# An adaLN layer (linear attention, then an int8-style FFN) on eight cores: row round trips moved to GpSimd's queue, staged weight pieces consumed in another order, FFN scales turned by TensorE

## The reference

```python
mod = (silu(c) @ wmod).reshape(8, 6, 1, 1024)
sa, ca, ga, sb, cb, gb = mod[:, 0], ..., mod[:, 5]
ga = (2 * (ga >= 0) - 1) * max(|ga|, 0.25)          # gb likewise
h = layernorm(x) * (1 + ca) + sa
q = relu(h Wq^T) / 8 ; k = relu(h Wk^T) / 8 ; v = h Wv^T ; u = silu(h Wu^T)   # 16 heads of 64
o = srms_norm(q @ (k^T v)) * u                      # k^T v summed over all 2048 tokens
x = x + ga * (o Wo^T)
h = layernorm(x) * (1 + cb) + sb
# per-token int8 quantization of h, per-row int8 quantization of the FFN weight, integer matmul
x = x + gb * ((h_q Wf_q^T) * h_scale * w_scale + bias)
```

## Time and profile before

| what | value |
|---|---|
| median of 3 runs | 490.98 us (487.46, 490.98, 512.98) |
| the profiled execution, its own time | 486.76 us |
| its span, slowest core (5) | 484.3 us |
| spans of the 8 cores | 467.4 to 484.3 us |
| PE busy | 397.9 us (82%) |
| DVE busy | 279.1 us (58%) |
| ACT busy | 231.4 us (48%) |
| POOL busy | 80.8 us (17%) |
| HBM read, written | 70.36 MB, 24.67 MB |

### The profile page before, as it was taken

How to read it: one execution, slowest core, us unless ns; L and a number is a source line. 1 busy time by engine, 2 the same in 40 slices (tenths; PEclk the granted TensorE clock), 3 DMA queues, 4 the chain that set the end, 5 groups by cost and what they waited for, 6 DMA issues and landing times.

```text
span 484.3 us, 6412 instructions; the slowest of 8 cores (467.4 to 484.3 us)
## 1 busy us (share of the span) xinstructions
PE 397.9 (82%) x2052; PEld 185.2 (38%) x2052; DVE 279.1 (58%) x492; ACT 231.4 (48%) x327; POOL 80.8 (17%) x136
## 2 busy tenths in 40 slices
PE   3234499999999982878978199989999989998994
PEld 0121244455454440324433044434344434444441
DVE  3565751647206656478557256556476645765885
ACT  4342153764662310776486253374844467643431
POOL 3222310515000000000022002121122122022321
PEclk9985789999999995989999789998999999999999
DMA  7999899593996999979999605634526554265787
GB/s 224 272 279 278 212 203 294 220 292 127 231 244 203 320 301 271 204 213 387 355 110 125 162 0 88 131 67 108 87 65 122 120 88 104 72 130 89 92 140 158
DMA packets 21185, 87.03 MB, mean 180 GB/s; under 512 B 4257, under 2 KB 4257, under 8 KB 16290
## 3 DMA queue, kind: packets, MB, share of 16 engines
q1 hardware_dynamic: 13666, 58.33, 39.5%
q0 software_dynamic: 7488, 28.31, 34.4%
HBM read 70.36 MB, written 24.67 MB: 196 GB/s over the span
## 4 chain that ended last, share of the span: by engine, by line
PE 38%; DMA 30%; DVE 11%; ACT 9%; issue 8%; SPq 2%; POOL 1%; DVEq 0%; ACTq 0%; POOLq 0%
PE pb L360 33%; DMA rows<-ws_c 7%; DMA wa<-wmod_a 7%; DMA stage<-wmod_b 5%; DMA row_g<-rows 5%; DMA xr<-x_tm 4%; DVE stage L427 3%; SPq L46 2%; ACT rn L677 2%; ACT osq L667 2%; PE pb L386 2%; PE pb L675 1%; ACT xq L777 1%; DVE wm_c L485 1%; DMA silr<-rows 1%
## 5 line engine op out<-in xcount | busy, mean ns | idle before, releaser
L360 PE MATMUL pb<-wo_s,u_s 128*128 128x512 bf16 x256 | 62.5, 398 | 1.4 <-DVE u_s L657 1.4
L360 PE MATMUL pb<-fq,xqT 128*128 128x512 bf16 x256 | 60.1, 379 | 2.6 <-ACT xqT L789 2.3
L360 PE MATMUL pb<-h,wq_s 128*128 128x512 bf16 x256 | 61.6, 385 | 0.0
L360 PE MATMUL pb<-h,wu_s 128*128 128x512 bf16 x256 | 61.5, 386 | 0.0
L360 PE MATMUL pb<-wv_s,h 128*128 128x512 bf16 x256 | 58.5, 379 | 0.0
L360 PE MATMUL pb<-wk_s,h 128*128 128x512 bf16 x208 | 45.7, 379 | 0.0
L427 DVE SCALAR_TENSOR_TENSOR stage<-stage,silr 128x1024 f32<-128x1024 f32 x32 | 37.6, 1222 | 11.6 <-DMA stage<-wmod_b 11.6
L682 DVE SCALAR_TENSOR_TENSOR q_s<-rn,pb 128x512 bf16<-128x512 f32 x32 | 21.9, 687 | 37.5 <-ACT rn L680 37.1
L360 PEld LDWEIGHTS pb<-wo_s,u_s 128*128 128x128 bf16 x256 | 25.9, 102 | 34.2 <-issue 7.7
L360 PEld LDWEIGHTS pb<-h,wq_s 128*128 128x128 bf16 x256 | 25.3, 99 | 29.6 <-issue 1.9
L360 PEld LDWEIGHTS pb<-h,wu_s 128*128 128x128 bf16 x256 | 25.1, 99 | 29.0 <-issue 1.4
(11 more groups left out here) (91 smaller groups left out, 551.9 us busy)
## 6 DMA issues: line engine op xcount, KB each, us to landing
stage<-wmod_b SPq DMA_DIRECT2D x16, 1024.0 KB, 9.0
xr<-x_tm SPq DMA_DIRECT2D x21, 512.0 KB, 5.3
wa<-wmod_a SPq DMA_DIRECT2D x8, 1024.0 KB, 31.2
out_tm<-row_gbb SPq DMA_DIRECT2D x4, 2048.0 KB, 29.0
out_tm<-xr POOLq DMA_DIRECT2D x15, 512.0 KB, 8.3
out_tm<-h POOLq DMA_DIRECT2D x15, 512.0 KB, 5.6
xr<-x_tm POOLq DMA_DIRECT2D x8, 512.0 KB, 17.2
stage<-wo SPq DMA_DIRECT2D x4, 1024.0 KB, 17.8
```

Source lines behind the costliest of these rows:

```text
L360: t = PE.do(lambda e, dc=dc: e.matmul(pb[bank][:], lhs(dc), rhs(dc), start=(dc == 0), stop=(dc == NC - 1)), *after, each(dc) if each else ...
```

## The change

Five edits go together.

1. `put` and `get` are issued from POOL instead of SP, and no longer inside `mod_fin` and `piece`: `row(0, row_g)` stands after `stats(15)` in V1, `row(1)` and `row(2)` between the halves of `wq` and `wu`, row 3 and 4 after K2's loop, before the second half of `wu`.
2. The stage stream's order is ga, sb, cb, wo, gb, ffn. `mod()` stands in every round of V0 and V1 and in the first four of K2: 8 pieces in V0, 8 in V1 (the first four each behind a `stats`), 4 in K2.
3. `xhat(12..15)` moves from the rounds 0-3 to 4-7 of K2, `transp(3,..)` from the rounds 0-3 to 2-5 of V2.
4. `ffn_quant(0..3)` is called in K3 (rounds 0-3) and `ffn_transp(0..3)` in V3 (rounds 0-3, each behind its `vproj`); the other four quants stand in the units 8-11, the other four transposes in the units 12-15. A one-column Ln on ACT stands at the end of phase A.
5. `last_row` turns `ws_c` by a matmul with an f32 identity, copies it to `ws_t` (8 partitions x 128) on DVE and puts 8 runs of 512 bytes, from POOL.

```diff
-    AT = {"ga": 0, "sb": 4, "wo": 8, "cb": 12, "gb": 16, "ffn": 20}
+    AT = {"ga": 0, "sb": 4, "cb": 8, "wo": 12, "gb": 16, "ffn": 20}
...
-        order = [[NC, 128], [1, NC]] if k < 5 else [[1, 128], [128, NC]]
-        put_tok[k] = SP.dma(sl_p[k], bass.AP(d_rows, k * D, order), col[:], *after, scattered=k > 4)
+        put_tok[k] = POOL.dma(sl_p[k], bass.AP(d_rows, k * D, [[NC, 128], [1, NC]]), col[:], *after)
...
-        row_tok[k] = SP.dma(sl_g[k], row[:], bass.AP(d_rows, k * D, [[0, 128], [1, D]]),
-                            put_tok[k], *after)
+        row_tok[k] = POOL.dma(sl_g[k], row[:], bass.AP(d_rows, k * D, [[0, 128], [1, D]]),
+                              put_tok[k], *after)
...
+    def row(v, dst, *after):
+        put(v, mod_c[v], col_tok[v])
+        get(v, dst, *after)
...
+    t_idf = DVE.do(lambda e: e.tensor_copy(out=id_f[:], in_=id_b[:]), t_const)
...
-    mods[8:8] = [lambda c=c: wo_piece(c) for c in range(4)]
+    mods[12:12] = [lambda c=c: wo_piece(c) for c in range(4)]
...
-        if n > 3:
-            mod()
+        mod()
...
-        else:
-            mod()
-    for h in range(2):
-        load_w("wq", wq, h, wa_free[NC - 1])
+        if n == 3:
+            row(0, row_g)
+        mod()
+
+    load_w("wq", wq, 0, wa_free[NC - 1])
+    row(1, row_sb)
+    load_w("wq", wq, 1)
+    row(2, row_cb)
+    load_w("wu", wu, 0)
     for n, (hf, j) in enumerate(eight):
         kproj(2, hf, j)
         if n == 0:
             kvprod(1, 3)
         if n < 4:
-            xhat(12 + n)
-        mod()
+            mod()
+        else:
+            xhat(8 + n)
+    row(3, row_g, fold_tok[0])
+    put(4, gbb_c, col_tok[3])
+    get(4, row_gbb)
+    load_w("wu", wu, 1)
     for n, (hf, j) in enumerate(eight):
         vproj(2, hf, j)
         if n >= 5:
             kvprod(2, n - 5)
-        if n < 4:
-            transp(3, n)
-        mod()
-    for h in range(2):
-        load_w("wu", wu, h, wa_free[NC - 1], st_tok[AT["gb"] + 3])
+        if 1 < n < 6:
+            transp(3, n - 2)
     for n, (hf, j) in enumerate(eight):
         kproj(3, hf, j)
         if n == 0:
             kvprod(2, 3)
-    fquant = [lambda ec=ec: ffn_quant(ec) for ec in range(NC)]
+        if n < 4:
+            ffn_quant(n)
     for n, (hf, j) in enumerate(eight):
         vproj(3, hf, j)
+        if n < 4:
+            ffn_transp(n)
         if n >= 5:
             kvprod(3, n - 5)
+    ACT.do(lambda e: e.activation(out=warm[:], in_=halfc, func=AF.Ln), t_half)
...
-        put(5, ws_c, fw_tok[NC - 1])
+        t = PE.do(lambda e: e.matmul(pb[7][0:NC, 0:128], ws_c[:], id_f[:], start=True, stop=True),
+                  fw_tok[NC - 1], t_idf, b7[0])
+        b7[0] = t = DVE.do(lambda e: e.tensor_copy(out=ws_t[:], in_=pb[7][0:NC, 0:128]), t)
+        put_tok[5] = POOL.dma(sl_p[5], bass.AP(d_rows, 5 * D, [[128, NC], [1, 128]]), ws_t[:], t)
         get(5, silr, col_tok[3])
...
-        if fquant and n > 5:
-            fquant.pop(0)()
-        if n > 7:
+        if 7 < n < 12:
+            ffn_quant(n - 4)
+        if n > 11:
             ffn_transp(n - 8)
```

More of the change, by code:

```diff
@@ L38, in do, with dma @@
         return (self.sem, self.n)
-    def dma(self, slot, out, in_, *after, add=False, scattered=False):
+    def dma(self, slot, out, in_, *after, add=False):
         slot.n += 16
         how = {"accum_op": ALU.add} if add else {}
-        if scattered:
-            how["allow_slow_non_contiguous"] = True
         self.items.append(([t for t in after if t is not None],
@@ L145, in build_nc @@
     mod_c = [sb(f"mod_c{v}", [128, NC]) for v in range(4)]
+    id_f = sb("id_f", [128, 128])
+    ws_t = sb("ws_t", [NC, 128])
+    warm = sb("warm", [128, 1])
     sgn_c = sb("sgn_c", [128, NC])
@@ L240, in build_nc @@
     wa_free = {}
-    stream = ([(d_wb, (0 * NC + 2 * c) * D, 4 * NC * D) for c in range(4)]
-              + [(d_wb, (1 * NC + 2 * c) * D, 4 * NC * D) for c in range(4)]
+    stream = ([(d_wb, (v * NC + 2 * c) * D, 4 * NC * D) for v in range(3) for c in range(4)]
               + [(d_wo, 2 * c * D, NC * D) for c in range(4)]
-              + [(d_wb, (2 * NC + 2 * c) * D, 4 * NC * D) for c in range(4)]
               + [(d_wb, (3 * NC + 2 * c) * D, 4 * NC * D) for c in range(4)]
               + [(d_fw, 2 * c * D, NC * D) for c in range(4)])
-    AT = {"ga": 0, "sb": 4, "wo": 8, "cb": 12, "gb": 16, "ffn": 20}
+    AT = {"ga": 0, "sb": 4, "cb": 8, "wo": 12, "gb": 16, "ffn": 20}
     def load_stage(n, *after):
@@ L456, in mod_fin @@
                                                         op0=ALU.subtract, op1=ALU.mult), t)
-        put(v, m, t)
         if v == 3:
@@ L460, in mod_fin @@
                        t, t_const)
[L461 to L465, removed]
+        col_tok[v] = t
+    def row(v, dst, *after):
+        put(v, mod_c[v], col_tok[v])
+        get(v, dst, *after)
     def wo_piece(c):
@@ L558, in piece @@
         mod_piece(v, c)
-        if c == 2 and v:
-            get(v - 1, ROWS[v - 1])
         if c == 3:
```

## The result

The changed kernel takes 496.5 us (median of 4 runs, 494.6 to 498.4). The kernel before took 490.4 us beside it; the ratio is 1.014, with an interval of 1.008 to 1.021. Medians here are of all runs of a kernel; ratios and intervals leave out the runs of a slower state that the chip sometimes falls into. The forecast was 495 us, no change that 2% would tell, with more chance for slower than for faster. The profiled execution has a span of 492.8 us on core 3; the spans of the cores are 484.0 to 492.8, where they were 467.4 to 484.3. On average a core takes 12.1 us longer (488.9 against 476.9), the slowest 8.5 us.

The account below looks back on a forecast made before the run. The stage stream, not PE, was taken to end phase A, with the scales' round trip the second long wait. 486.8 + 23.5 - 2.8 - 5.1 - 11.4 = 491.0, +4.2; from the 491.0 median that gives 495 us, range 481 to 507.

Parts of the forecast that it names:

- E: Landing of the first ffn piece in the stage stream: forecast at 188, bounds 181 to 196.
- V3's wait replaces the wait for `kv_bd`: In V3 PE stands 28 us for `wi` 0; first `ohead` at E + 26.2 = 214.2, +23.5 us.
- rival 1: The stage stream runs better, E 174 to 183: 481 to 490 us; chance 0.18.
- 491.0 + (E - 183.8): The forecast's short form: whole time in us as a function of the first ffn piece's landing.
- added ahead of it: Row 2 and the first half of `wu`, 2.5 MiB ahead of the first ffn piece, delay it 8.3 us.
- the 7.5 us of idle DMA time: Idle DMA time left by DVE's new order, out of 15.7 us unused before.
- From E to the first `ohead`: End of phase A: second ffn piece 7.5 us behind the first, first `ohead` at E + 26.2.
- Row 0 through POOL: Row 0's trip from POOL takes 4 us for the put, 7 for the get; `row_g` lands at 144 to 147.
- The rival of a starved trip: Row 0's trip through POOL is slow beside DVE's work: `row_g` near 153, E = 196, 503 us; chance 0.27.
- `xhat(15)` late, hidden: In V2 the late `xhat(15)` would cost PE about 3 us, hidden in V3's 28 us stall.
- Units 0 to 15: First unit loop: -2.8 us in units 0 and 1, -5.1 us in units 8 to 15.
- The scales' trip: At `gws`, PE's 9.0 us wait and 2.4 us of half clock behind it go: -11.4 us.

Follow-up runs that it names:

- e8: The changed kernel with the first half of `wu` loaded behind row 4, beside the second half, instead of ahead of the ffn pieces: 492.0 us, ratio 0.987.
- e1: The changed kernel with all eight FFN quants and transposes back in units 6 to 15 of the first unit loop: 477.0 us, ratio 0.983.
- e5: e1 with `row(0, row_g)` asked for in round 0 of V1, ahead of the statistics: 475.3 us, ratio 0.979.
- e2: The kernel before with edit 5 alone (scales turned by PE, put as 8 runs, put and get from POOL): 479.1 us, ratio 0.987.
- e11: The kernel of e2 run again on another set's chip, beside the changed kernel: 480.4 us, ratio 0.989.
- e9: The changed kernel with all eight transposes in units 8 to 15, none in V3, and quants 0 to 3 still in K3: 491.6 us, ratio 0.985.

## Why the prediction was right, step by step

The forecast time, 495 us, is 1.5 us from the measured 496.5. In part that is luck. The terms for V3's stall held in kind, but the moment E on which the sum is built came 6 us earlier than forecast, and what followed E took 8.5 us longer.

- **V3's wait replaces the wait for `kv_bd`: right.** First wait 19.1 us, forecast 28 (20 to 30 as its sign), with the first transposition at 185.9 instead of 187 to 194; first `ohead` at 216.8 on the slowest core, forecast 214.2, inside 208 to 220. Over all cores it moved from a mean of 186.4 to 211.8, +25.4 against +23.5.
- **When the first ffn piece lands: wrong, 6 us too late.** It was issued at 172.13 and took 9.9 us, so E is 182.0 where 188 was forecast; on the eight cores it is 174.6 to 182.4. No core is in the forecast's 184 to 193.8. All are in the range of rival 1 (174 to 183), and one is under the 175 that was named as a sign of being wrong. Rival 1 priced this at 481 to 490 us, and so does "491.0 + (E - 183.8)", with 489: condition and price don't go together. Two things made E early. First, the baseline was core 5's, whose last gb product began at 184.3; on core 3 it began at 181.0 before and at 179.4 after. Second, the 8.3 us "added ahead of it" weren't ahead: the get of row 2 was issued at 177.4 and the first half of `wu` at 178.0, behind that piece, and they landed at 186.5 and 195.8. A third worked the other way: the 7.5 us of idle DMA time were 13 us on core 3 (34 x 0.18 + 38 x 0.18), where 16.2 were counted before, so 3 us were taken back and not 8. The new order saved 8 us of it up to 122 (0.59 to 0.82 busy), and lost 5 behind it (0.94 to 0.82), where `row_g`'s trip holds up the stream. These give 188 - 3.3 - 3.2 = 181.5, as an estimate.
- **From E to the first `ohead`: 34.7 us, forecast 26.2.** The second ffn piece is the main part: 12.8 us between quant 0's start and quant 2's, forecast 7.5, and above the bound of 10; e8 shows the cause. DVE was still busy with gb when E came (1.1 us). And PE's clock fell behind both waits, not one, so the last transposition came 2.0 us after its block was ready (203.1 and 201.1). With the early E this cancels in part: quant 3 was to end at 200.7, and ended at 201.1. The wait for `wi` is shorter than forecast by 5 us for E and by 4 because V3 itself began at 164.9, not at 160.8 as on core 5.
- **Row 0 through POOL: right.** 4.6 us for the put's landing and 5.0 from the get's issue to Wo's first product; forecast 4 + 7, `row_g` at 144 to 147. Its first product was at 142.0 to 147.8 on the eight cores. The rival of a starved trip, for which the Trainium skill's "SBUF — State Buffer", section "SBUF: two separate sides", spoke, didn't happen to this row, with DVE idle beside it. POOL's small operations did slow down beside DVE's products, 1.04 and 1.34 us at 122.9 against 0.22 and 0.57. No trace here shows a starved DMA of POOL's: the slow puts of rows 1 to 3 landed 0.2 to 0.9 us behind the load in front of them, on all eight cores, so they were slow because that load was.
- **`xhat(15)` late, hidden: right**, but 0.7 us on core 3, 1.3 on others (e1), not 3; in e5 it was 5.6.
- **Units 0 to 15: -6.8 us, forecast -7.9.** From the first `ohead` to the group loop 37.8 us (216.77 to 254.54), before 44.6. The first eight took 15.2 as forecast; the other eight 22.6 instead of 21.5, since quant 4 began only at 240.9, 8.9 us into unit 8.
- **The scales' trip: -10.8 us on the slowest core, forecast -11.4** (group loop 238.3 instead of 249.0 us), but -7.5 in the mean of the cores, as in e2 and e11 (-7.4 and -7.6). The sum's weak spot: on cores 2 and 4 PE had waited 2.4 and 2.2 us there, not 9.0, so they gain little. This is most of why the mean of the cores rose by 12.1 us and the slowest span by 8.5. I read the terms on the core that was slowest before, and those of it were special in both: its stream was late, and its row was late.
- **The sum**: in the span +26.1 - 6.8 - 10.8 = +8.5, forecast +4.2; in the medians +6.1, by the ratio +7.

## What to carry to other kernels

Work moved to an earlier place in a hand-written order helps only if its data can be there. Count the bytes that must land ahead of it, casting loads by what they read, and compare with the engine's own timetable: here some 24.5 MiB (the 27 of the prediction less the 2.5 that came behind), 82 us at 0.30 MiB/us, were due in 71 us. And a load issued later than the piece that you wait for isn't ahead of it: it delays the pieces behind. When a round trip through memory is slow, look first at the size of its elements and at what stands ahead of it in its queue; then at who stands behind the engine that waits for it. And read a gain on every core: what the slowest core wins, the second slowest may not. Where the baseline scatters, keep a second kernel that repeats well beside every set of runs; the split of a cost can turn round with the yardstick, as it did here for e9.

## What the runs showed of the hardware that I had not expected

- The landing of a put of 4 KB depends on what stands ahead of it in its own queue far more than on what runs beside it. From POOL it took 1.6 us with nothing ahead and the DMA engines idle (share 0.01), 4.7 us with nothing ahead and the engines 0.61 busy, and 10.5 and 21.0 us behind half a casting load each (share 0.89 and 1.00). In the last two it landed 0.2 and 0.6 us after the load in front of it.
- 1024 elements of 4 bytes beside the fill took 22.1 us from POOL's queue, where the same 4 KB as 8 runs of 512 bytes took 7.8 (e2). From SP's queue, behind the fill, it was 34.7 against 12.1. They also slowed the fill: its last DMA took 44.3 and 51.3 us with the elements, 28.8 and 29.5 without.
- In the kernel before, DMA-bound stretches differ by 10 us between cores that do the same work: `row_g`'s first product came at 137.0 to 146.9. The three cores with the earliest row also ended first.
